# A routed tile's down product a slot later on TensorE, with three buffers for its transposed operand

## The reference

```
x = x + layernorm(attention(layernorm(x)))          # 16 heads in 4 groups, RoPE, causal
x = x + layernorm(ffn(layernorm(x)))
ffn(x)    = x + mlp(x, shared) + sum over the top 2 of 16 experts of value * mlp(x, expert)
mlp(x, .) = (silu(x @ wg) * (x @ wu)) @ wd          # wg, wu: 256x128, wd: 128x256
```

## Time and profile before

| | us |
|---|---|
| median of three runs | 2489.6 |
| the profiled execution | 2487.5 |
| its span, first to last instruction | 2485.7 |
| TensorE busy | 2295.1 |
| VectorE busy | 1931.7 |
| GpSimd busy | 1693.8 |
| ScalarE busy | 1397.1 |
| TensorE waiting for the copy of `hid_t` at L1696 | 34.1 |

### The profile page before, as it was taken

One profiled execution on the slowest core, in us unless ns is written; L12 is line 12 of the kernel. 1 busy time (PEld: TensorE's weight loads), 2 busy tenths in 40 slices (PEclk: granted clock), 3 DMA queues, 4 the chain that ended last, 5 costly groups with the idle time before them and its releaser, 6 DMA issues.

```text
span 2485.7 us, 57906 instructions
## 1 busy us (share of the span) xinstructions
PE 2295.1 (92%) x17882; PEld 1478.2 (59%) x17882; DVE 1931.7 (78%) x5140; ACT 1397.1 (56%) x3208; POOL 1693.8 (68%) x2893
## 2 busy tenths in 40 slices
PE   5999999999999999999999999998779899999997
PEld 2565555555555555555555555554568687777754
DVE  6788888888888888888988888876455454676778
ACT  1566666656666566665656665665344444444444
POOL 4557777677776777766767766753656566777776
PEclk7899999999999999999999999999899999999999
DMA  4544445554455544444443444332344466788877
GB/s 132 136 137 148 149 128 157 160 155 141 134 155 155 162 138 131 147 138 145 120 130 108 139 136 130 112 99 74 112 143 148 132 188 201 250 274 279 268 257 255
DMA packets 289486, 391.76 MB, mean 158 GB/s; under 512 B 28000, under 2 KB 237920, under 8 KB 289056
## 3 DMA queue, kind: packets, MB, share of 16 engines
q1 hardware_dynamic: 263168, 316.72, 42.8%
q0 software_dynamic: 26016, 71.34, 7.9%
HBM read 186.84 MB, written 182.75 MB: 149 GB/s over the span
## 4 chain that ended last, share of the span: by engine, by line
PE 73%; DVE 9%; issue 6%; POOL 4%; ACT 3%; DMA 2%; another core or an unknown queue 2%; SPq 0%; ACTq 0%; POOLq 0%; DVEq 0%
PE ps_out L872 11%; PE ps_a L858 10%; PE ps_d L842 10%; PE bank L1682 9%; PE ps_d L888 6%; PE bank L1696 5%; PE ps_d L895 4%; PE ps_a L860 4%; PE ps_d L844 4%; DVE roped_q L1123 3%; PE bank L1663 2%; DVE negmax L1108 2%; ACT proj L1030 2%; PE bank L1690 1%
## 5 line engine op out<-in xcount | busy, mean ns | idle before, releaser
L985 ACT ACTIVATE probs<-ps_a 128x512 f32<-128x512 f32 (+1 forms) x1408 | 712.4, 558 | 441.5 <-PE ps_a L860 350.1
L1108 DVE TENSOR_REDUCE negmax<-ps_d 128x2 f32<-128x768 f32 (+3 forms) x768 | 773.5, 1032 | 145.0 <-PE ps_d L844 79.6
L858 PE MATMUL ps_a<-qs,ks 99*128 99x512 bf16 (+3 forms) x2048 | 516.3, 303 | 18.3 <-ACT probs L985 14.5
L842 PE MATMUL ps_d<-ks,qs 96*128 96x128 bf16 (+3 forms) x2048 | 491.1, 306 | 26.2 <-DMA qs<-q_stack_dram 11.0
L844 PE MATMUL ps_d<-mask_max,ident_bf 128*128 128x128 bf16 x2048 | 397.1, 223 | 0.0
L860 PE MATMUL ps_a<-mask_exp,ident_bf 128*128 128x128 bf16 x2048 | 389.2, 221 | 0.0
L1593 POOL DMA_INDIRECT y_dram<-ysb,to_row x286 | 285.9, 1000 | 97.2 <-issue 50.2
L872 PE MATMUL ps_out<-probs,va 128*32 128x512 f32 (+3 forms) x4096 | 331.4, 442 | 3.0 <-DVE by_token L1158 3.0
L842 PEld LDWEIGHTS ps_d<-ks,qs 96*128 96x128 bf16 x2048 | 203.3, 99 | 197.0 <-DVE negmax L1108 42.7
L858 PEld LDWEIGHTS ps_a<-qs,ks 99*128 99x128 bf16 x2048 | 199.6, 98 | 200.1 <-issue 71.9
L769 POOL DMA_INDIRECT sorted_dram<-h,slot x256 | 267.5, 1045 | 66.4 <-issue 65.4
(11 more groups left out here) (208 smaller groups left out, 4245.5 us busy)
## 6 DMA issues: line engine op xcount, KB each, us to landing
qs<-q_stack_dram SPq DMA_DIRECT2D x128, 384.0 KB
rows<-sorted_dram SPq DMA_DIRECT2D x286, 129.0 KB
y_in<-y_dram SPq DMA_DIRECT2D x32, 1024.0 KB
q_stack_dram<-q_parts SPq DMA_DIRECT2D x64, 384.0 KB, 3.0
x_in<-in_x SPq DMA_DIRECT2D x32, 512.0 KB, 4.2
q_stack_dram<-q_parts SPq DMA_DIRECT2D x64, 256.0 KB, 3.2
h_dram<-h SPq DMA_DIRECT2D x32, 512.0 KB
h<-h SPq DMA_DIRECT2D x32, 512.0 KB
```

The costliest lines, as they stand in the source:

```text
L842: pe.matmul(ps_d[:, number % 2, at:at + width], qs[0:KR, b % 2, h, j * P:(j + 1) * P], ks[0:KR, b % 2, g, 0:width], start=True, stop=False)
L858: pe.matmul(ps_a[:, number % 3, at:at + width], ks[0:KM, b % 2, g, j * P:(j + 1) * P], qs[0:KM, b % 2, g * HG + h0 + k, j * P:T], start=Tr ...
L985: act.activation(probs[:, at:at + nh * width], ps_a[:, number % 3, 0:nh * width], ACT.Exp) \
L1108: dve.tensor_reduce(negmax[:, g // 2, j, at:at + nh], src, AX_X, ALU.max, negate=True) \
```

## The change

The down product of a tile is put a slot later on TensorE; what depends on it is put a slot later as well: VectorE's name_rows and take_y, and GpSimd's store_y. The buffer `hid_t` gets a third copy, and ScalarE's wait for a free one is adapted. The total of slots, the loads' lead (`AHEAD`), the buffers for rows and the places of the final steps stay.

```diff
-        hid_t = sb("hid_t", [P, 2, P])
+        hid_t = sb("hid_t", [P, 3, P])
@@ gpsimd_experts, turn(t)
-            if 3 <= t < ALL_TILES + 3:
-                store_y(t - 3)
+            if 4 <= t < ALL_TILES + 4:
+                store_y(t - 4)
@@ tensor_experts, down(t)
-            pe.matmul(ps_y[t % 2][:, 0:D], hid_t[:, t % 2, :], wd[:, expert[t], :], start=True, stop=True) \
+            pe.matmul(ps_y[t % 2][:, 0:D], hid_t[:, t % 3, :], wd[:, expert[t], :], start=True, stop=True) \
@@ tensor_experts, turn(t)
-            if 2 <= t < ALL_TILES + 2:
-                down(t - 2)
+            if 3 <= t < ALL_TILES + 3:
+                down(t - 3)
@@ scalar_experts, take_hidden(t)
-            if t >= 2:
-                act.wait_ge(y_done, t - 1)
-            act.copy(hid_t[:, t % 2, :], ps_h[:, 0:P]).then_inc(hid_t_ready, 1)
+            if t >= 3:
+                act.wait_ge(y_done, t - 2)
+            act.copy(hid_t[:, t % 3, :], ps_h[:, 0:P]).then_inc(hid_t_ready, 1)
@@ vector_experts, turn(t)
-            if 2 <= t < ALL_TILES + 2:
-                name_rows(t - 2)
-                take_y(t - 2)
+            if 3 <= t < ALL_TILES + 3:
+                name_rows(t - 3)
+                take_y(t - 3)
```

## The result

The changed kernel took 2506.78 us (median of six runs) against 2487.72 for the kernel before beside it: ratio 1.0079, 95% interval 1.0053 to 1.0104, 19 us slower. One of the six executions of the kernel before took 4533.7 us and is left out of the ratio. The forecast of 2486.6 us was wrong, and the time lies above its range. The profiled execution took 2494.3 us (span 2492.5), one of the quickest of its six.

The account below looks back on a forecast made before the run. The prediction took TensorE's products to bound the kernel, plus 34.1 us of waits at L1696 for ScalarE's hid_t copy. 2487.5 - 8.0 + 5.0 = 2484.5, with 2.1 to the timed median 2486.6 us; range 2477 to 2499.

Parts of the forecast that it names:

- later loads of rows: SP's rows loads, released a slot later by take_y, come late in the stretch with final steps: 5.0 us cost.
- later down product, held ScalarE: TensorE's waits at L1696 for ScalarE's hid_t copy shorten: 11.0 less 0.9 and 2.1, 8.0 us gained.
- of the four places with some margin I give 0.6 each: Rows loads in the final-step stretch at four places without a seen wait: 0.6 us cost each.
- upper bound of 13.0: Cost of later rows loads if all seven places move by the full 1.86 us: 13.0 us.
- the forecast's 2.6: Cost at the three places where a wait for rows is seen, 0.87 us each: 2.6 us.
- the shorter shift: If SP's queue never runs dry, a rows load lands only 0.87 us later, with the burst, instead of 1.86.
- What moves with it, at nothing: VectorE's naming and take_y and GpSimd's store_y go a slot later with the same durations, at no cost.
- A hold is shortened by the smaller of its wait and 0.43.: At L1696, TensorE runs ahead of a held ScalarE by one down product: 11.0 us over 28 waits.
- (a): Rival: rows loads decide, 1.86 us at all seven places, 13.0 us cost, gains only 3: 2499.6 us; chance 0.17.
- (b): Rival: the hid_t wait only moves to L1690, nothing saved and 5.0 us paid: 2494.6 us; chance 0.10.
- (c): Rival: shorter idle pieces near 1754 and 2083 keep TensorE's clock at 2.4 GHz, 4 us more gained: 2482.6; chance 0.12.
- (d): Rival: the whole 34.1 us wait for hid_t at L1696 goes: 2460.5 us; chance 0.04.

Follow-up runs that it names:

- e1: The changed kernel again, with nothing altered; ratio 1.0086 to the kernel before.
- e4: The changed kernel with the naming of rows put back in its old slot, take_y still a slot later; ratio 1.0041 to the kernel before.
- e3: The kernel before with seven buffers for rows instead of eight; ratio 1.0063 to the kernel before.
- e17: The changed kernel with nine buffers for rows and the naming in its old slot, on chip 6; ratio 0.9975 to the kernel before.
- e18: The kernel before with nine buffers for rows instead of eight, on chip 6; ratio 0.9974 to the kernel before.
- e9: The kernel before again, with nothing altered, on chip 5; ratio 1.0019 to the kernel before.
- e10: The changed kernel again, with nothing altered, on chip 5; ratio 1.0103 to the kernel before.
- e16: The changed kernel again, with nothing altered, on chip 6; ratio 1.0083 to the kernel before.
- e2: The changed kernel with nine buffers for rows instead of eight, on chip 15; ratio 1.0007 to the kernel before.
- e11: The changed kernel with nine buffers for rows instead of eight, on chip 5; ratio 1.0015 to the kernel before.
- e15: The changed kernel with nine buffers for rows instead of eight, on chip 14; ratio 1.0007 to the kernel before.
- e12: The changed kernel with the last tile's down product, naming and take_y back in their old slot; ratio 1.0107 to the kernel before.
- e5: The kernel before with nine buffers for rows instead of eight, on chip 11; ratio 0.9983 to the kernel before.
- e13: The kernel before with nine buffers for rows instead of eight, on chip 14; ratio 0.9989 to the kernel before.
- e6: The changed kernel with nine buffers for rows and the naming in its old slot, on chip 11; ratio 0.9985 to the kernel before.
- e14: The changed kernel with nine buffers for rows and the naming in its old slot, on chip 14; ratio 0.9979 to the kernel before.

## Why the prediction was wrong

**The sum, term by term.** Ratios near 2490 us, in us of 2487: the changed kernel is at 1.0079, 1.0086, 1.0103 and 1.0083 (mean 1.0088, +21.9). With nine buffers of rows it is at 1.0007 and 1.0015 (mean 1.0011), with the naming early as well at 0.9975. Each step from one to the next takes out one part of the change, and the parts add up:

| term | predicted | measured |
|---|---|---|
| later loads of rows | +5.0 | 1.0088 - 1.0011 = 0.0077, 19 us |
| later naming of rows | 0 | 1.0011 - 0.9975 = 0.0036, 9 us (on the quicker chip 6.6; e1 less e4, with eight buffers, 11) |
| later down product, held ScalarE | -8.0 | 0.9975 - 1.0000 = -0.0025, -6.2 us |
| sum | -3.0 | +21.9 |

The loads' term has two more measures: e3, where a slot's lead is taken from the kernel before and nothing else moves, 0.0063, 16 us; and e4 less e17, with the naming early in both, 0.0066, 16 us. The single terms are good to some 5 to 7 us each: the intervals of the ratios are 0.002 to 0.003 to either side, and they come from different chips, each against the kernel before on its own.

**The step that failed first: "of the four places with some margin I give 0.6 each", in the term for the later loads.** The mechanism was named rightly, its size was not: 5.0 us were taken, 16 to 19 measured, over the upper bound of 13.0 as well. In the places where the kernel before waits for rows, the growth stays within the forecast's 2.6: from 3.7 us to 4.3 in after and to 6.0 in e1. The rest is in places where it doesn't wait at all: five with 8.8 us in after, nine with 14.4 in e1. Their margins were taken as small costs because no wait was seen. Two of the five and five of the nine are loads right behind the burst and ahead of the y load, like the one at 2274.84, a kind that the sum doesn't have; one, of 1.76 us at 2025.77, lies ahead of the final steps, where a load of h2 stands in the queue. The clock falls behind such waits, which the sum doesn't have either.

The condition on which the shorter shift was chosen, that the queue never runs dry, holds in the trace, but "the queue had 2.5 MB in it" is what SP had issued and not what was left. Here is what the DMA engines moved in after, in 40 slices of 0.65 us from 2228 to 2254:

```profile
GB/s 410 334 347 377 387 274 218 41 202 8 92 318 202 0 0 0 0 105 360 351 181 85 191 326 347 317 394 388 376 421 403 403 391 368 383 226 220 120 132 0
```

The burst goes out from 2238.7 and brings it to 360. From 2241.0 to 2242.9 it is 181, 85 and 191, though by 2242.3 SP had issued 1.8 MB (the burst and two loads of rows) and no more than 0.7 MB had moved. So the queue still held over 1 MB and moved it slowly; why, no run here shows. By the ring order rule of the Trainium skill ("DMA: Bandwidth & Descriptors", "Queues, rings and completion order") the cost would have been 2.6. The trace doesn't speak against the order; the error is in which loads had a margin. The same page's advice to issue early and wait late pointed the right way. And e18 shows that visible waits don't measure the margins: a ninth buffer is worth 0.26% (6.5 us, interval 2.5 to 10) to the kernel before, which showed only 3.7 us of waiting for rows.

**The step that failed second: "What moves with it, at nothing", VectorE's naming of rows among it.** "With the same durations" was the error. Beside GpSimd's add (2.35 us) a naming stands still: each one of over 0.3 us in before, after and e1 ends within 0.03 us of the end of an add, and lasts 0.7 to 3.1 us. Counting the namings of over 0.3 us instead of 0.15: 3 with 7.6 us together in before, 5 with 11.1 in e9; 9 with 18.2 in after, 12 with 25.7 in e1, 10 with 20.0 in e10 and 10 with 21.1 in e16. The naming's slot alone doesn't set that number: e3, with the old slot and seven buffers, has 9 with 20.9 us, and e2 and e11, with the late slot and nine, have 6 each with 16.0 and 13.6. What the catches cost ahead of the last tile isn't shown.

Their `named` count is what SP's loads ask for, and at the end of the tiles they stand in the chain itself: 2.2 us on VectorE, and in after, e2, e11, e15 and e16 the clock falls behind the wait as well, in e1 and e10 it does not. With the naming early the end stage is 114.4 us (e4, e17) as in before. So some 5 of the 9 us are at the last tile. The last tile is caught in each trace of the late naming but e12's, which puts it back, and in none of the others: in its new slot the naming stands behind VectorE's statistics and starts as the add does.

The Trainium skill ("SBUF — State Buffer", "SBUF: two separate sides") states the rule: a VectorE operation with two inputs in SBUF and a GpSimd operation that reads SBUF exclude each other on a shared port, and the one that starts second waits for the whole of the other. The traces agree at the last tile (2.31 us beside 2.35), for an operation of one element in each partition too. They don't bear out who goes first: the naming of 3.08 us at 2234.68 is shown as starting 0.69 us ahead of its add (2235.37 to 2237.73).

**The gain: "A hold is shortened by the smaller of its wait and 0.43."** The timing bears out its size, 6.2 us (1.2 to 11.2) against 8.0, and the traces the movement. L1696 has 0.3 us of waits left; L1690 has 22.7 us in 20 places, but only 15.7 in 11 of them for the copy of `hid_t`, where I had said about 24 in 22. All waits of L1663, L1690 and L1696 but those for rows sum to 45.2 us (mean of before, e9, e18, e3; 37.4 to 51.8) and to 40.6 with the later down (mean of after, e1, e10, e16, e2, e11, e4, e17; 30.2 to 51.4). So 4.7 us less by the traces, with a spread of several times that. Part of what L1696 lost is at L1690 under another name: the wait for VectorE's `hid` is 2.6 to 2.9 us in before and e9, and 3.9 to 15.3 in six traces of late naming, 6.6 and 3.4 with the naming early. Why VectorE is later there no run shows. That 0.43 for each hold is the mechanism of the gain isn't shown either: on the quicker chips, where L1696 waits for `hid_t` in five places (e5, e13) and the rule allows 2.2 us at most, 3.6 and 5.0 were gained.

**Rivals.** (a), the rows loads decide, had the terms 13.0 and a gain of 3 and gave 2499.6; with the naming's 9 us it gives 2508.6, beside the 2506.8 measured. It is the nearest, partly by luck, since its cost and its gain are both too small. Its chance of 0.17 was too low. (b), nothing is saved, has the timing of e17, e6 and e14 against it. (c): near 1754, where the kernel before runs at 0.50, after runs at 1.00, but from 1730 to 1870 the clock is 0.95 in after and 0.91, 0.91 and 0.92 in e1, e10 and e16, against 0.92 in before and e9; so no gain is borne out, and behind the waits for rows and at the end the clock now falls where it didn't. (d) is refuted by L1690's waits.

**The signs that I named.** Waits for rows over 12 us: 13.1, and this by my own words makes the forecast wrong. From 1870 to 1925 full: right. From 1925 to 2000 "idles 3 us less": 7 less in that trace. Rows late between 1870 and 2000: none; the steady slot's 3.5 us held there.

**Open.** By what path the later down product gains on chips with few holds; whether it would still gain with the loads a slot earlier (ten buffers); what of the naming's 9 us lies ahead of the last tile; and why a ninth buffer gives the kernel before more on chip 6 (6.5 us) than its waits for rows.

## What to carry to other kernels

A buffer that a later stage sets free is part of the move: ask at once for one more, or price it by all loads whose margin isn't measured. A wait of zero in the trace is no margin: measure from the load's landing to its use. To tell what one part of a change is worth, compare kernels in which every other release falls in the same slot. Before a step is costed at nothing because it "only goes a slot later", look at what runs on the other engines in that slot. The best of the versions here keep the naming where it was and add a buffer: 0.9974 to 0.9989, with the down product early or late.

## What was not expected of the hardware

The same kernel takes 2484 to 2492 us on three chips and 2373 to 2375 on two. Part of the difference is before the tiles, which start at 1728 to 1734 us on the former and at 1663 to 1667 on the latter; the tiles 0 to 60 then take 145 to 157 us against 121 to 124. What the traces show there are holds like that of the earlier trace rows, where an engine stands idle with no queue of its core behind it. ScalarE's waits from 1660 to 2300, in before and in e13 (chip 14):

```profile
ACT gate L1803 <- issue: 41.9, 77, 2.4
ACT gate L1803 <- remote: 19.1, 10, 4.6
```

```profile
ACT gate L1803 <- PE bank L1682: 132.2, 263, 1.3
ACT hid_t L1809 <- PE bank L1690: 124.8, 262, 5.5
```

In e13 "issue" is 0.5 us, once, and "remote" doesn't occur. At L1696, the target of this change, e13 waits 7.1 us, and e18, the same kernel on chip 6, 24.7 (10.4 for `hid_t` and 14.3 put down to issue): most of it was the chip's and not the schedule's. What makes one chip hold its engines and another not, no run here shows.
